# Attention scores computed twice, the second time keys by queries with the negated maxima inside the product

## What is computed

```python
scores = jnp.einsum('bhqd,bhkd->bhqk', Q_, K_) / D_HEAD ** 0.5
if use_causal_mask:
    scores = jnp.where(causal, scores, jnp.float32(-1000000000.0))
sim = jax.nn.softmax(scores, axis=-1)
att = jnp.einsum('bhqk,bhkd->bhqd', sim, V_)
```

## Time and profile before

| what | value |
|---|---|
| median of 3 runs | 1738.43 us (1736.29 to 1738.66) |
| span of the profiled execution | 1734.3 us |
| PE busy | 1664.1 us, 96% |
| ACT busy | 1357.1 us, 78% |
| DVE busy | 1313.4 us, 76% |
| POOL busy | 533.5 us, 31% |

### The profile page before, as it was taken

One profiled execution on the slowest core, in us unless ns is written; L12 is line 12 of the kernel. 1 busy time (PEld: TensorE's weight loads), 2 busy tenths in 40 slices (PEclk: granted clock), 3 DMA queues, 4 the chain that ended last, 5 costly groups with the idle time before them and its releaser, 6 DMA issues.

```text
span 1734.3 us, 54906 instructions
## 1 busy us (share of the span) xinstructions
PE 1664.1 (96%) x21232; PEld 1438.0 (83%) x21232; DVE 1313.4 (76%) x3355; ACT 1357.1 (78%) x4026; POOL 533.5 (31%) x1288
## 2 busy tenths in 40 slices
PE   6789999999999999999999999999999999999976
PEld 6577888888888888888888888888888888888765
DVE  3577778887778888877888887788888778888542
ACT  2367888888888888888888888888888888888763
POOL 1333233332323333232333333233333323333110
PEclk9899999999999999999999999999999999999998
DMA  7000000000000000000000000000000000000000
GB/s 266 8 8 8 8 8 12 6 10 9 11 12 11 11 6 10 9 11 11 12 11 8 8 8 11 12 11 11 10 5 9 10 11 11 9 5 5 5 4 10
DMA packets 26176, 26.92 MB, mean 16 GB/s; under 512 B 2240, under 2 KB 25024, under 8 KB 25792
## 3 DMA queue, kind: packets, MB, share of 16 engines
q1 hardware_dynamic: 25920, 23.41, 4.1%
HBM read 19.21 MB, written 4.19 MB: 13 GB/s over the span
## 4 chain that ended last, share of the span: by engine, by line
PE 88%; DVE 7%; issue 2%; ACT 1%; POOL 1%; DMA 0%; DVEq 0%; SPq 0%; POOLq 0%; ACTq 0%
PE ring L581 26%; PE ring L587 22%; PE ring L569 18%; PE score L637 6%; PE ring L678 5%; PE ring L755 3%; PE ring L765 2%; DVE conv L1237 2%; PE ring L668 2%; PE ring L816 1%; DVE conv L1231 1%; PE score L628 1%; DVE neg_max L1144 1%; PE ring L748 1%; ACT exps L954 1%
## 5 line engine op out<-in xcount | busy, mean ns | idle before, releaser
L954 ACT ACTIVATE exps<-score,neg_max 128x128 f32<-128x128 f32 x1808 | 491.4, 409 | 112.7 <-DVE neg_max L1144 112.7
L1144 DVE TENSOR_REDUCE neg_max<-score 128x4 f32<-128x512 f32 x452 | 289.8, 683 | 118.9 <-PE score L637 118.8
L1400 POOL TENSOR_TENSOR stat<-stat 128x1 f32<-128x1 f32 x224 | 128.8, 575 | 698.3 <-DVE stat L1116 698.3
L960 ACT COPY weights<-ring 128x512 f32<-128x512 f32 x452 | 257.3, 658 | 44.0 <-PE ring L569 42.3
L569 PE MATMUL ring<-const,exps 128*128 128x128 f32 x1808 | 240.1, 275 | 11.6 <-ACT exps L954 7.9
L569 PEld LDWEIGHTS ring<-const,exps 128*128 128x128 f32 x1808 | 210.2, 142 | 33.9 <-ACT exps L954 15.8
L1231 DVE SCALAR_TENSOR_TENSOR conv<-raw,vectors,conv 128x128 f32<-128x128 f32 x576 | 168.5, 348 | 6.8
L581 PE MATMUL ring<-actT,w_q 128*128 128x128 f32 x1024 | 138.0, 278 | 2.5 <-ACT actT L926 2.5
L637 PE MATMUL score<-K,QB 32*128 32x128 f32 x3616 | 135.2, 283 | 0.5 <-issue 0.5
L637 PEld LDWEIGHTS score<-K,QB 32*128 32x128 f32 x3616 | 113.8, 188 | 21.9 <-issue 21.7
L926 ACT COPY actT<-ring 128x256 f32<-128x256 f32 x224 | 86.4, 386 | 56.3 <-PE ring L569 56.3
(11 more groups left out here) (165 smaller groups left out, 3472.5 us busy)
## 6 DMA issues: line engine op xcount, KB each, us to landing
cT<-in_ctxT SPq DMA_DIRECT2D x32, 128.0 KB, 2.1
x_in<-in_x SPq DMA_DIRECT2D x32, 128.0 KB, 2.0
out<-result SPq DMA_DIRECT2D x32, 128.0 KB, 2.1
row_all<-in_rows SPq DMA_DIRECT2D x1, 1420.0 KB, 10.2
w_in<-in_in_proj SPq DMA_DIRECT2D x1, 1288.0 KB, 7.2
w_k<-in_k SPq DMA_DIRECT2D x4, 256.0 KB, 6.1
w_v<-in_v SPq DMA_DIRECT2D x4, 256.0 KB, 6.3
w_q<-in_q SPq DMA_DIRECT2D x4, 256.0 KB, 6.8
```

The source lines that it names most:

```text
L954: last = run(exps[:, n, h * P:(h + 1) * P], of, ACT.Exp, bias=neg_max[:, m, h:h + 1])
L960: nc.scalar.copy(weights[:, buffer(it, a_, l, t, WEIGHT_BUFFERS), half * 4 * P:(half + 1) * 4 * P], t_[:, :]).then_inc(read, 1)
L1144: nc.vector.tensor_reduce(neg_max[:, m, 4 * half:4 * half + 4].rearrange("p (b h) -> p b h", b=each), score[:, first:first + each, 0:4 // ...
L1400: tt(stat[:, l, 10:11], stat[:, l, 2:3], stat[:, l, 4:5], ALU.pow).then_inc(S[done], 1)
```

## The change

Attention 1 keeps its steps but the last: `values1` now has the transposed exponentials as weights, 32 queries at a time, and V with its column of ones (33 columns) as the moving side, 32 products, so that the result has queries on partitions; DVE's reciprocal runs over 128x8, and a new task `ctxT` transposes the result (two transpositions) for `Wo`.

A square attention is now:

- `quads` as before, with DVE's maxima written to `maxima_at`, to the columns 32r and 32r+16 of two blocks, so that a transposition puts them into the rows that `QB` has left zero.
- `mT`: two transpositions of `maxima_at` on PE, two ACT instructions that put the rows into `shift_rows`, and one POOL addition of 128x512 that adds them to `QB`.
- `KE`: keys with a one in the spare row of the other head, two ACT instructions for attentions 2 and 3 (from `K2`), four instead of two for attention 4.
- `quadsT`: the scores again, with keys as weights and `QB` as the moving side, so keys on partitions and the negated maximum of each query inside the sum. The causal mask is laid again, turned.
- `exps`: one ACT exponential for each bank, 128x512, with no bias, four in all. No transposition, no copy, no `attT`, no `back`.
- `values`: exponentials as weights, 32 queries at a time, and V with its ones (17 columns) as the moving side, 64 products, four at a time on the four groups of columns. Queries lie on partitions, and DVE reads the bank at once.

Each `score` bank is now handed on by DVE's reduction after `quads`, and by ACT's exponential after `quadsT` and in attention 1. All places, shifts and spare products are new; tasks of one sample now reach over about four periods.

```diff
-    conv0=10.153, conv1=1.914, silu=8.942, pairs=2.154,
+    Q4=-65.6542, V1=-102.572, V2=-84.1886, V3=-76.0867, V4=-69.3427, Wo=-88.1363, Y=-96.0555, am=-150.6689, conv0=-141.1603,
...
-SPARE = {("turn0_0", 0): 5, ("turn0_1", 0): 4, ("bias", 0): 7, ("xhatT", 0): 17, ("pairs", 0): 18, ("Y", 0): 5, ("uT", 0): 4,
-         ("turn1_0", 0): 5, ("Wo", 0): 6, ("Y", 1): 4, ("x4T", 0): 5}
+SPARE = {("mT0", 0): 11, ("values0", 0): 9, ("xhatT", 0): 7, ("pairs", 0): 18, ("Y", 0): 7, ("uT", 0): 6, ("xnT", 1): 5}
...
+            def free(it, kind, a_, l, r):
+                n = it.number(UNIT_AT, kind, a_, l)
+                if n:
+                    semaphore, value = bank_used(*UNITS[n - 1], r)
+                    pe.wait_ge(S[semaphore], value)
...
             def quads(it, a_, l):
...
+                for c in range(DC):
+                    for f in range(2):
+                        e, at = 1 - f, (2 * c + f) * P
                         for r, rows_of in enumerate(ROWS_OF):
+                            if not masked and at == 0:
+                                free(it, "quads", a_, l, r)
+                            keys = K2[rows_of, l, c, :] if a_ in (2, 3) else KE[rows_of, l, c, e, :]
+                            last = mm(score[:, r, at:at + P], QB[rows_of, l, c, e, :], keys,
...
+            def turn_maxima(it, a_, l):
+                pe.wait_ge(S["maxima"], maxima_done(it, a_, l, TILES - 1))
+                flip(it, f"mT{a_}", l, maxima_at[:, maxima_buffer(it, a_, l), :, :].rearrange("p c k -> p (c k)"), DC)
+
+            def quadsT(it, a_, l):
+                masked = a_ in (2, 4)
+                pe.wait_ge(S[f"shift{a_}"], 1 if a_ == 0 else nth(it, l))
+                if a_ in (2, 3):
+                    pe.wait_ge(S[f"KE{a_}"], nth(it, l))
+                if masked:
+                    lay_causal(it, "quadsT", a_, l, 1)
...
+                            last = mm(score[:, r, at:at + P], KE[rows_of, l, c, e, :], QB[rows_of, l, c, e, :],
...
             def values(it, a_, l):
...
-                for four in range(H16 // TILES):
-                    for r in range(TILES):
-                        h = TILES * four + r
-                        t = h % 8 // 4
-                        last = mm(output[ROWS_OF[r], four * P:(four + 1) * P], V2[:, l, h, :],
-                                  exps_of(t, heads_of(a_, t).index(h)), start=True, stop=True)
...
+                for c in range(DC):
                     for r in range(TILES):
+                        for e in range(2):
+                            h, at = 8 * c + 2 * r + e, (2 * c + e) * P
+                            for q, queries in enumerate(ROWS_OF):
+                                last = mm(output[queries, h * (DH16 + 1):(h + 1) * (DH16 + 1)],
+                                          weights[:, buffer, r, at + queries.start:at + queries.stop], V2[:, l, h, :],
+                                          start=True, stop=True)
...
+            def exponential(it, a_, l):
+                for r in range(TILES):
+                    act.wait_ge(S[f"scores{r}"], nth_unit(it, "quadsT", a_, l))
+                    run(weights[:, turned_buffer(it, a_, l), r, :], score[:, r, :], ACT.Exp).then_inc(S["exps"], 1)
...
+            def shifts(it, a_, l):
+                t, read = filled(it, f"mT{a_}", l)
+                for e in range(2):
+                    last = run(shift_rows[:, :, e, :], t[:, 0:D].rearrange("p (c k) -> p c k", c=DC), ACT.Copy,
+                               scale=spare_row[:, e:e + 1])
+                last.then_inc(read, 1)
...
+            def maxima(it, a_, l):
+                for r in range(TILES):
+                    dve.wait_ge(S[f"scores{r}"], nth_unit(it, "quads", a_, l))
+                    nc.vector.tensor_reduce(
+                        maxima_at[:, maxima_buffer(it, a_, l), :, 32 * r:32 * r + 17:16],
+                        score[:, r, :].rearrange("p (c f k) -> p c f k", c=DC, f=2),
+                        AX_X, ALU.max, negate=True).then_inc(S["maxima"], 1)
...
+                def shift(a_, l):
+                    evacuated(it, f"mT{a_}", l)
+                    tt(QB[:, l, :, :, :], QB[:, l, :, :, :], shift_rows[:, :, :, :], ALU.add).then_inc(S[f"shift{a_}"], 1)
```

637 lines of the change are left out of this document (353 added, 284 removed).

## The result

| | before | after |
|---|---|---|
| median of the runs, us | 1738.5 | 1813.5 (1812.7 to 1813.7) |
| ratio to before, 95% interval | 1 | 1.0433 (1.0418 to 1.0448) |
| span of the profiled execution, us | 1734.3 | 1811.9 |
| PE busy, us | 1664.1 | 1655.2 |
| DVE busy, us | 1313.4 | 1341.2 |

The account below looks back on a forecast made before the run. PE was taken as the bound, 50.5 us a sample: 1734.3 - 64 (PE work) + 22 (waits) = 1692 us of span, with 4.1 us for the median 1696 us (1682 to 1712, chance 0.45); 8-in-10 range 1660 to 1745.

Parts of the forecast that it names:

- The price of a group with 17 columns: Values: four products starting together, run through twice in float32; taken as 0.035 us each, 3.9 us for 112.
- the sum on PE: PE's work for a sample: 10.8 us removed, 8.9 added, 1.96 us less, 63 us for 32 samples.
- The last rival: `values2` to `values4`: narrow products are not cheap, issue allows 0.064 us a group, 41 us more on PE; 1778 us; chance 0.15.
- the 8-column rows: `q_first` on PE, same 32 columns of weights: 0.15 us for 4 groups, 0.038 each, nearest guide to 17 columns.
- the sign that the prediction had named for itself: PE: forecast wrong if the array pays for each change between full, row and column products, three more a sample.
- DVE's term: DVE's work for a sample: maxima keep their shape, reciprocal shrinks; 41.0 us become about 39.5, 80% as now.
- the two places that I had named: PE waits 0.1 to 0.3 us before `quadsT4`; the maxima's way from `mT3` to `quadsT3` has 1.2 us to spare.
- The term of 22 us for waits: PE's waits in the middle double from 0.7 to 1.4 us a sample, 22 us more.
- The rival on DVE's pace (1722): DVE sets the pace in half of the period, late maxima and normalisations cost 1.5 us a sample; 1722 us; chance 0.2.

Follow-up runs that it names:

- experiment 1: Changed kernel with the square attentions' values as 16 wide products of 128 moving columns again, V as weights; 1738.8 us, ratio 0.9995.
- 11: Changed kernel with exponentials and values of the square attentions in bfloat16, one pass instead of two; 1716.2 us, ratio 0.9874.
- 2: Kernel before the change with each wide product of its square attentions' values cut into four of 32 columns; 1845.5 us, ratio 1.0612.
- experiment 4: Changed kernel with all 64 products of the values of a square attention done twice, same result; 2236.0 us, ratio 1.2858.
- 5: Changed kernel with values of every attention as products of 64 columns of weights on two column groups, half the instructions; 1813.6 us, ratio 1.0448.
- 7: Changed kernel with values on 64 columns of weights, and POOL's addition to QB on 32 columns instead of 512; 1779.5 us, ratio 1.0237.
- 8: Changed kernel with values on 64 columns of weights, and POOL's addition to QB and log decays each cut into four; 1783.4 us, ratio 1.0263.
- 10: Changed kernel with its narrow values, and POOL's addition to QB made small, on 32 columns instead of 512; 1783.7 us, ratio 1.0242.

## Why the prediction was wrong

**The account by sample.** From the first product of attention 1's values (L668, L741) in one sample to that in the next, mean of 25 samples in the middle of each trace, in us. "At half" is what the half clock took at the most.

| | period | idle, issue | idle, other waits | PE busy | of it, at half |
|---|---|---|---|---|---|
| before | 50.57 | 0.00 | 0.32 | 50.23 | 0 |
| changed | 54.14 | 2.71 | 0.85 | 50.54 | 0.8 |
| changed, the 16 samples at full clock | 53.16 | 2.33 | 0.93 | 49.87 | 0 |
| experiment 1 | 51.56 | 0.17 | 1.71 | 49.61 | 0 |

The forecast was that the period falls by 1.96 us of work and rises by 0.7 us of waits, to 49.3. It rose by 3.57. The difference of 4.8 us is 2.7 for issue, 1.6 of PE's own work (0.36 saved and not 1.96), 0.7 for the clock, and 0.2 less in other waits. 4.8 x 32 are 154 us. What the span has beside 32 such periods, at its two ends, went the other way, from 116 to 79 us, and the forecast had nothing for that; 154 - 37 leaves 117 us, the whole miss. That it comes out to the microsecond is luck: the parts are good to some 0.1 us a sample.

**The steps that held.** Values 1.13 to 1.20 (forecast 1.1), second scores 1.11 (1.11), the mask 0.37. The price of a group with 17 columns was 0.037 us (taken: 0.035). ACT fell by (1357.1 - 1096.6)/32 = 8.1 us a sample (8).

**The step that failed: the sum on PE had no term for the supply of its instructions.** It was made of durations, start to start, and took for granted that PE has its next instruction. The last rival came near: it named the place (`values2` to `values4`, long runs) and the cause (issue), and asked whether the 8-column rows were runs "of 16 only, which may have been waiting ready". But it put the limit into the price of a group, where it is not; the price was right and the blocks were late. A stall for each block of 250 instructions doesn't show in any run of 16, nor in the 64 records of the earlier trace rows. The numbers to see it were in the page: 173 packets, 21232 products and as many loads. They say what is in a block; what it costs to pass one too fast no row of before showed, since its blocks had 10 us each. Size: 91.6 - 5.1 = 86 us of idle time. The half clock (1.2 and not 2.4 GHz) goes with it: it was granted for 44 us between 90 and 1650 us instead of 4, and ten of these eleven stretches began at most 2.0 us after a stall or wait of over 0.5 us, as this one, right behind the stall of 1.56 us:

```profile
876.70:880.10 3.40, 3.40 (x9) 1.99 (x8) 2.83 (x7) 0.66 (x2) 2.91 (x3) 0.50 0.00 0
```

**The second term: PE's own work, 1.6 us a sample.** One period shows it too: from 871.40 to 925.10 are 53.7 us; without the 1.56 for issue, the 0.87 for DVE and the 1.7 us lost at half the clock, 49.6 us of work are left, and the period of before had 50.3 without its one wait of 0.19. New rows cost more than taken: some 0.6 us for the values, a part of it the time around a stall that counts as busy (those of attention 1, with 33 columns, 0.76 us for 16 groups, 0.048 each and not 0.035) and 0.35 for the transposed maxima and `ctxT` (0.28 a pair, taken as 0.22). And rows that did not change became longer: PE's projections with 128 columns (L581 before, L630 now) take 15.3 us a sample and took 14.5. A projection of eight products takes 0.995 us from start to start right behind a row or column product (868.76 to 869.75 above; the mean of 84 such rows) and 0.95 in the mean behind others; before, 32 such rows took 0.995 too, and the others 0.91. This is the sign that the prediction had named for itself, "if the array pays for each change between full, row and column products". It stays in experiment 1, without stalls and at full clock: 49.6 us of work.

**DVE's term was mis-sized.** "DVE's maxima keep their shape" was right and 39.5 us a sample wrong: 1341.2/32 = 41.9, since POOL's new additions and their places shut DVE out. Under this falls the wait at L618 for `res` (21.0 us), outside the two places that I had named, behind the convolution that had become longer. With the small addition the time fell by 30 us. Little of this is the shorter way of the maxima: PE waited 5.8 us for `QB` in all, 3.2 at L722 and 2.6 at L662.

**The term of 22 us for waits** had about the right size (0.53 us a sample, 17 us) for a wrong reason: at L662 and L722 PE waited for anything but issue for 8.6 us in the whole trace, and the wait for `res` came from the exclusion. So the 30 us of the exclusion lie mostly inside this term, not beside it. The rival on DVE's pace (1722) was half right: with supply out of the way, in experiments 1 and 11, PE waits for other engines for 1.7 and 1.8 us a sample, most of it for `res` from DVE.

What experiments show is the supply (1, 2, 4, 5 and 11) and the exclusion (7, 8 and 10). That PE's own work was under-priced is read from the traces alone, and no run separated its parts.

## What to carry to other kernels

Count instructions as well as time: divide an engine's instructions, weight loads included, by its instruction packets, and ask of each stretch how long a block lasts. In this case, where a block was to pass in less than some 3.5 us, cutting a product into narrower ones for its price bought a stall, and halving the passes (a narrower type) helped twice. And before work goes to POOL, look which DVE instructions with two inputs in the SBUF it will lie beside. Cut POOL's long operations so that DVE gets in between, unless someone waits for the last piece; compare the duration of a whole group with that of another of its shape, since a group that is always shut out looks normal. And take the waits out of both sides when a period is held against a forecast: otherwise a term that failed hides behind one that did not come.

## What the runs showed of the hardware that I had not expected

- No block of some 250 PE instructions was passed in less than 3.28 us: this was the shortest distance of two packets in the changed kernel; in experiment 4, with 368 packets, the shortest was 3.37 us, and one in ten was at 3.53 or less.
- Products of 17 columns: with 32 columns of weights on four column groups, 9 ns for a load and its product, 37 for four; with 64 on two, 31 ns, and a pair in 58; with 128, 112 ns. The same 128 columns of weights cost three times as much in one piece as in four.
- POOL shuts DVE out by the instruction: DVE's 0.48 us became 2.05 beside one of 1.90 us, and the mean of its group fell from 0.82 to 0.54 when that one was cut into four.
- Eight products of 128x128 took 0.995 us right behind products on 32 rows or 32 columns, and 0.91 (before) to 0.95 (changed) behind full ones, mean of each.
- In the kernel with 128 columns of weights and 17 of data PE was busy for 1535.3 of 1560 us and got a mean clock of 0.89 there; with 32 columns, four times as many products for the values and PE busy for 1455.5 us the clock was 0.99, and in the kernel before, busy for 1538.4 us, 1.00. What of its activity decides this stays open.
